# Bias times edge count between two graph layers: from additions on VectorE to one-row products on TensorE

## What is computed

```python
h = relu(layernorm(x))
# layer 0
ef  = (relu(edge_attr @ We1 + be1) @ We2 + be2) * sigmoid(ts @ Wt + bt)
msg = relu(concat([h[src], ef]) @ Wn1 + bn1) @ Wn2 + bn2
x   = x + segment_sum(msg, dst) + h
# layer 1
h   = relu(layernorm(x))
agg = segment_sum(h[src], dst)
x   = x + relu(relu((h + agg) @ W1 + b1) @ W2 + b2)
```

## Time and profile before

| | |
|---|---|
| median of 3 runs | 2862.56 us (2857.91 to 2863.95) |
| the profiled execution | 2860.48 us, span 2858.7 us, mean granted TensorE clock 0.892 |
| busy share of the span: PE, DVE, ACT, POOL | 84%, 69%, 35%, 73% |
| the stage between the layers, from the last sum to the scales | 2089.1 to 2123.9 us |

### The profile page before, as it was taken

One profiled execution on the slowest core, in us unless ns is written; L12 is line 12 of the kernel. 1 busy time (PEld: TensorE's weight loads), 2 busy tenths in 40 slices (PEclk: granted clock), 3 DMA queues, 4 the chain that ended last, 5 costly groups with the idle time before them and its releaser, 6 DMA issues.

```text
span 2858.7 us, 51515 instructions
## 1 busy us (share of the span) xinstructions
PE 2413.2 (84%) x14584; PEld 1509.5 (53%) x14585; DVE 1970.6 (69%) x4063; ACT 1001.7 (35%) x1000; POOL 2098.3 (73%) x2125
## 2 busy tenths in 40 slices
PE   5698899888889888988998898998846988877887
PEld 3455455545555555555554554554443666655665
DVE  7887767776777777777777777889886443444443
ACT  4344444444444444444443443443251111111113
POOL 7777777777777777777777777777737777777772
PEclk8899999999999999999999998999876788777878
DMA  6455554554545454555445544454314554455442
GB/s 224 117 161 158 155 156 155 155 154 155 155 154 155 154 155 155 154 155 155 154 154 155 154 155 150 155 156 144 103 67 151 163 163 149 135 163 162 150 131 69
DMA packets 229337, 426.09 MB, mean 149 GB/s; under 512 B 82703, under 2 KB 141664, under 8 KB 228992
## 3 DMA queue, kind: packets, MB, share of 16 engines
q0 software_dynamic: 74672, 152.51, 20.4%
q1 hardware_dynamic: 103152, 177.42, 18.5%
q10 hardware_dynamic: 51266, 93.34, 9.2%
HBM read 363.63 MB, written 59.43 MB: 148 GB/s over the span
## 4 chain that ended last, share of the span: by engine, by line
POOL 39%; PE 25%; issue 17%; DVE 10%; DVEq 5%; DMA 2%; ACT 1%; POOLq 0%; ACTq 0%; SPq 0%
POOL big L541 39%; PE ps L943 10%; PE ps L854 4%; PE ps L812 3%; PE ps L822 2%; DVE arena L1203 2%; PE ps L833 2%; DVE nodes L1203 2%; PE ps L933 1%; DVEq L1137 1%; PE ps L803 1%; DMA big<-table,idx 1%; DVEq L1183 1%; DVEq L1200 1%; DVEq L1203 1%
## 5 line engine op out<-in xcount | busy, mean ns | idle before, releaser
L541 POOL DMA_INDIRECT big<-table,idx x2080 | 2032.6, 977 | 658.1 <-issue 631.0
L656 ACT ACTIVATE big<-big 128x1024 f32<-128x1024 f32 x196 | 207.3, 1058 | 1014.7 <-DVE big L1152 1009.5
L854 PE MATMUL ps<-nodes 128*128 128x500 bf16 x1280 | 384.1, 415 | 180.1 <-DVE nodes L1203 179.2
L1152 DVE TENSOR_TENSOR big<-ps,big 128x1024 f32<-128x1024 f32 x196 | 239.8, 1224 | 328.6 <-DMA big<-table,idx 327.4
L1203 DVE TENSOR_SCALAR nodes<-iota_k,win_off,nodes 128x500 bf16<-128x500 f16 x1280 | 461.9, 413 | 0.0
L812 PE MATMUL ps<-arena,we 128*128 128x512 f32 x784 | 442.5, 692 | 11.8 <-DVE arena L1172 5.4
L833 PE MATMUL ps<-hot,big 128*128 128x64 f32 x3136 | 372.1, 272 | 1.6 <-DVE hot L1158 1.6
L833 PEld LDWEIGHTS ps<-hot,big 128*128 128x128 f32 x3136 | 365.9, 192 | 1.9 <-ACT big L656 1.7
L735 ACT ACTIVATE arena<-ps 128x490 f32<-128x490 f32 x96 | 100.1, 1043 | 557.0 <-PE ps L857 531.3
L854 PEld LDWEIGHTS ps<-nodes 128*128 128x128 bf16 x1280 | 95.6, 101 | 374.6 <-DVE nodes L1203 311.5
L646 ACT ACTIVATE arena<-ps,cols 128x1024 f32<-128x1024 f32 x196 | 218.5, 1115 | 202.7 <-PE ps L803 146.7
(11 more groups left out here) (147 smaller groups left out, 2382.3 us busy)
## 6 DMA issues: line engine op xcount, KB each, us to landing
arena<-in_ew SPq DMA_DIRECT2D x196, 512.0 KB
arena<-in_ea SPq DMA_DIRECT2D x196, 256.0 KB, 2.9
counts_d<-arena ACTq DMA_DIRECT2D x192, 245.0 KB
acc<-counts_d ACTq DMA_DIRECT2D x15, 2940.0 KB
big<-table,idx POOLq DMA_INDIRECT x2080
table<-big SPq DMA_DIRECT2D x7, 672.0 KB, 3.0
idx<-in_src SPq DMA_DIRECT2D x260, 4.0 KB, 1.6
xs<-in_x SPq DMA_DIRECT2D x7, 448.0 KB, 6.2
```

The lines of the kernel that those rows point to most:

```text
L541: pool.indirect_dma_start(to(u, q, t)[0:n], None, table, bass.IndirectOffsetOnAxis(ap=idx[0:n, u, at:at + 1], axis=0))\
L854: m = pe.matmul(to, hots[:, t, :], keys[:, t, :], start=False, stop=True, skip_group_check=True)
L1152: dve.tensor_tensor(msg[:, u % 2, :, :, :].rearrange("p q t d -> p (q t d)"), p_pre2, rows[:, u, :, :, :].rearrange("p q t d -> p (q t d)" ...
```

## The change

The bias additions on DVE go, with the seven multiplications on POOL, the count transfer on SP, the tile `count_n` and the four `biases` buffers. In their place:

- POOL copies the count row into a row `edge_counts` in partition 0, in which the 128 counts of a column lie side by side: seven copies of 7 x 128 elements. It waits for the last sum, no longer for a transfer.
- PE follows each of the 49 products by one with a single row, counts (1 x 128) by bn2 (1 x 128), in float32, which adds into the same PSUM buffer. Each group waits for its copy.
- SP waits for the last product before it loads the stored counts, as they overwrite the count row.

```diff
+        edge_counts = arena[0:1, at:at + N_PAD].rearrange("f (t p) -> f t p", t=NT)
...
             sp.wait_ge(acc_added, sweeps * NB)
-            sp.dma_start(count_n[:, :], acc[0:1, 1, 0:N_PAD].rearrange("a (p t) -> a p t", t=NT)).then_inc(counts_moved, 16)
-
-            sp.wait_ge(counts_moved, 16)
+            sp.wait_ge(upd_mm, NG)
             for i in (0, 1):
                 sp.wait_ge(c_stored[i], 16 + 16 * (NW0 // 2))
             load_sums(sp, 0)
...
-            pool.wait_ge(counts_moved, 16)
-            bn2_g = bn2_r[:, :].rearrange("p (a d) -> p a d", a=1).to_broadcast([P, GT, D])
+            pool.wait_ge(acc_added, sweeps * NB)
+            pool.sem_inc(pairs_begun, 1)
             for g in range(NG):
-                if g >= len(biases):
-                    pool.wait_ge(x1_chain, g - len(biases) + 1)
-                n = count_n[:, g * GT:(g + 1) * GT].rearrange("p (t a) -> p t a", a=1).to_broadcast([P, GT, D])
-                pool.tensor_tensor(biases[g % len(biases)], bn2_g, n, ALU.mult).then_inc(bias_made, 1)
+                pool.tensor_copy(edge_counts[:, g * GT:(g + 1) * GT, :], acc_group(g, 1)[0:1, :, :]).then_inc(counts_turned, 1)
             pool.tensor_copy(keys1, keys0).then_inc(keys_moved, 1)
...
                 if g >= 2:
                     pe.wait_ge(x1_made, g - 1)
+                pe.wait_ge(counts_turned, g + 1)
                 for u in range(GT):
-                    i = pe.matmul(p_prod[g % 2][:, u, :], stages[g % 2][:, u, :], wn2[:, :], start=True, stop=True)
+                    pe.matmul(p_prod[g % 2][:, u, :], stages[g % 2][:, u, :], wn2[:, :], start=True, stop=False)
+                    i = pe.matmul(p_prod[g % 2][:, u, :], edge_counts[:, g * GT + u, :], bn2_r[0:1, :], start=False, stop=True)
                 i.then_inc(upd_mm, 1)
...
-            def add_bias(g):
-                x_g = xs[:, g * GT:(g + 1) * GT, :]
-                dve.wait_ge(bias_made, g + 1)
-                dve.tensor_tensor(x_g, x_g, biases[g % len(biases)], ALU.add).then_inc(x1_chain, 1)
-
-            add_bias(0)
             for g in range(NG):
                 x_g = xs[:, g * GT:(g + 1) * GT, :]
                 dve.wait_ge(upd_mm, g + 1)
-                dve.wait_ge(x1_chain, g + 1)
                 dve.tensor_tensor(x_g, x_g, p_prod[g % 2], ALU.add).then_inc(x1_made, 1)
-                if g < NG - 1:
-                    add_bias(g + 1)
                 dve.wait_ge(x1_made, g + 1)
```

More of the change, by code:

```diff
@@ L122, in gnn_program @@
         rstd = sb("rstd", [P, NT])
-        count_n = sb("count_n", [P, NT])
         shift = sb("shift", [P, NT])
@@ L177, in gnn_program @@
         dense_edges = arena[:, at:at + NTILE]
+        edge_counts = arena[0:1, at:at + N_PAD].rearrange("f (t p) -> f t p", t=NT)
+        assert at + N_PAD <= sum(sizes) + 2 * BLK
         at += CB * CSUM
@@ L219, in gnn_program @@
         h_stages = [big[:, i * GT * D:(i + 1) * GT * D].rearrange("p (t d) -> p t d", t=GT) for i in (0, 1)]
-        biases = [big[:, i * GT * D:(i + 1) * GT * D].rearrange("p (t d) -> p t d", t=GT) for i in range(4)]
-        assert 4 * GT * D <= RROW
         half_at = RROW + 2 * TB * D - GT * D
@@ L304, in gnn_program @@
         acc_staged = sem("acc_staged")
-        counts_moved = sem("counts_moved")
-        bias_made = sem("bias_made")
-        x1_chain = sem("x1_chain")
         acc_zeroed = sem("acc_zeroed")
@@ L332, in gnn_program @@
         keys_moved = sem("keys_moved")
+        counts_turned = sem("counts_turned")
         sums_loaded = sem("sums_loaded")
```

## The result

The changed kernel takes 2903.97 us, the median of four runs between 2901.42 and 2907.02, beside 2863.26 us for the kernel before, now the median of four runs: a ratio of 1.0143, 95% interval 1.0127 to 1.0158. It is 40.7 us slower; 41 had been forecast.

The account below looks back on a forecast made before the run. VectorE was taken as the bound; TensorE's 98 products at 0.70 us, 68.6 us from 2093.97 us, plus 2.6 us of VectorE end at 2165.2 instead of 2123.9 us: 41 us more, 2904 us, range 2873 to 2914.

Parts of the forecast that it names:

- VectorE bounds, TensorE has 6 us of slack, 9 us to win: Stage between the layers: VectorE is the bound; without its bias additions it could end about 9 us earlier at most.
- A product with its change costs 0.70 us at half clock, 0.42 at full: TensorE's alternating 128-row and one-row products: 98 of them take 68.6 us at half clock, 41 us at full.
- TensorE starts as before, at 2093.97 us: Start of the stage: TensorE's branch past the skipped sweep loop sets it; the wait for GpSimd's first copy costs nothing.
- A change to 64 rows and one to a single row wait alike: TensorE's row changes: going from 128 rows to 64 or to one starts the next record 0.09 to 0.15 us late.
- Half clock for the whole stage: TensorE in the stage: pauses, 40% of the time without columns, keep the granted clock at 0.50; chance 0.62.
- the counting stretch: Cited evidence, 2188.2 to 2211.9 us: TensorE works through counts with pauses and was granted 0.50 for all 23.7 us.
- The full-clock rival: TensorE gets full clock after 4 to 5 us and keeps it: 15.7 us more, 2878 us; chance 0.22.
- No price for the change of rows: Rival: one-row products on TensorE follow like any other, 0.11 us a record: 3.7 us less, 2859 us; chance 0.12.
- GpSimd's copies at 0.80 to 2.53 us, hidden: Seven strided count-row copies, each 0.80 to 2.53 us, nearer the second; TensorE's wait on them costs nothing.
- SP's late load, hidden: SP's load of stored sums starts 2.6 us before the statistics end, is in about 7 us after, and costs nothing.
- VectorE waits some 7 us for a group: Sign in the profile after: VectorE waits for TensorE in six of seven groups, some 7 us each.
- The rest moves by the same amount: All behind the stage, scales, normalizing, table and gathers, moves by the same 41 us.

Follow-up runs that it names:

- the 64-row stream: Changed kernel with count products on 64 rows, alternating with 128: 2905.39 us begun cold; 2890.57 us begun warm behind 42 added 128-row products.
- the one-row run: Changed kernel with each group's seven 128-row products before its seven one-row products, plus 42 warming and 98 unbroken one-row products ahead of the first group: 2917.39 us.
- the grouped order: Changed kernel with each group's seven 128-row products first, then its seven one-row products, 2 changes of rows a group instead of 14: 2863.97 us, ratio 1.0014.

## Why the prediction was right, step by step

- *VectorE bounds, TensorE has 6 us of slack, 9 us to win.* Right: without the one-row products the stage lost 10.2 us.
- *A product with its change costs 0.70 us at half clock, 0.42 at full.* Right: 0.72 and 0.42 us. TensorE's stretch is 70.93 us where 68.6 were forecast. What made the sum 2.3 us too small is mostly the second record of a product: 0.34 us behind the first in the earlier trace rows, 0.38 us here. The weight loads of a product start together with its first record (PEld below), so they were not made ahead. The late start after a change was right, 0.35 us behind the last record for the forecast 0.21 + 0.15. TensorE's single records in the timeline of after show both:

```profile
2098.66 0.42 PE L904 MATMUL ps<-bn_r,arena 1*128 1x128 f32 x1
2099.00 0.50 PEld L903 LDWEIGHTS ps<-wn,big 128*128 128x128 f32 x2 [0.22 <-issue]
2099.00 0.58 PE L903 MATMUL ps<-wn,big 128*128 128x128 f32 x1
...
2099.38 0.42 PE L903 MATMUL ps<-wn,big 128*128 128x128 f32 x1
2099.73 0.58 PE L904 MATMUL ps<-bn_r,arena 1*128 1x128 f32 x1
```

  Against the 0.43 and 0.22 us of the products without a change, one change is worth 0.72 - 0.43 = 0.29 us at half clock and 0.42 - 0.22 = 0.20 at the full one.
- *TensorE starts as before, at 2093.97 us.* This term was too large by about as much. The first product stood 2093.97 - 2089.13 = 4.8 us behind ScalarE's first copy before and 2096.14 - 2093.23 = 2.9 us now; the branch began 0.8 us behind that copy then and 1.0 us ahead of it in this execution. So 2.3 us too little and 1.9 too much nearly cancel, and that the forecast met the median so closely is partly luck.
- *A change to 64 rows and one to a single row wait alike.* Right: 70.90 and 70.93 us. That the price could be avoided by using 96 or 128 rows was not in the prediction.
- *Half clock for the whole stage.* Right in its number, 0.50 over 70.93 us, and at most half right in its reason. The step laid it to the pauses, and the counting stretch stood for it. That a stream with pauses can stay cold fits the 64-row stream, cold against warm, but there the pauses are not parted from the 64 rows. And the prediction weighed only pauses: it did not see that one-row work loses the clock without any, as the one-row run did. With 56 changes instead of 98 the clock still stayed down. So the right level came in part from a reason that the runs don't bear out.
- *The full-clock rival's argument that the clock would stay once reached*. Wrong for this change (lost after 5.9 us), right for 64 rows (kept for 40.8 us). The Trainium skill, TensorE: Matmul & The Clock Gate, section Why this matters for your kernels, asks that TensorE be kept busy without a break and that long idle gaps be avoided; the prediction named the second alone. By the profile the one-row run met both, busy for 36.15 of 36.15 us, and was at half clock, so here the measurement decides against reading them as enough.
- *No price for the change of rows.* Refuted for 64 rows and for one; with 96 or 128 rows it is what happens, 2861 and 2860 us, near the 2859 of that rival.
- *GpSimd's copies at 0.80 to 2.53 us, hidden.* 1.76 us each, about the middle rather than near the upper end; the first was in 0.8 us before the branch was through.
- *SP's late load, hidden.* It started at 2167.15 us, 2.5 us before the statistics ended, as forecast. The first store of the table came 10.5 us after the statistics, at 2180.20 us, as before.

```profile
2180.20 0.34 SPq L471 DMA_DIRECT2D table<-big  x1
```

- *VectorE waits some 7 us for a group.* 7.55 us. *The rest moves by the same amount*: 41.7 us in the stage, 40.7 in the medians.

What stays open: how much of the 64-row stream's half clock in its cold run is due to the pauses and how much to the 64 rows, as no run of 64 rows without pauses began cold; how many rows between 1 and 64 are enough to keep the clock; where between 64 and 96 rows the change begins to cost; and when the grouped order reaches the full clock.

## What to carry to other kernels

Before small products are put between large ones on TensorE, look at the rows that both use: pad the small operand with zeros (96 and 128 rows were tried), or do all of one kind before the other. Padding brought the 41 us back in every run; the order did so in the median, but three of its runs were 15 to 19 us longer, and behind one-row work its clock stayed at half. Judge the granted clock of a stretch by its own row and not by PE's busy share, which was full at half clock throughout. And work that leaves the bound engine wins only what its new place leaves: VectorE's additions were worth 10 us here, and even in the cheap form TensorE's second products took 7 of them (a stage of 31.9 us, 2087.56 to 2119.49, beside 24.5 without bias and 34.8 before).

## What the runs showed of the hardware

- A dense run of one-row products, PE and its weight loads busy throughout, lost the full clock after 3.1 us; one with 64 rows kept it for 22 us.
- Groups of seven products on 128 rows and seven on one row were granted 1.00 from 3.6 us after a start behind 4.0 us of idleness, and 0.51 for 43 us behind a run of one-row products at half clock.
- One and the same stream (128 and 64 rows in turns) was granted 0.50 for 70.9 us when it began cold and 1.00 for 40.8 us when it began warm.
- A product of 96 rows behind one of 128 pays for no change (0.22 us from start to start at the full clock); one of 64 rows costs 0.20 us more, and so does one of a single row.
- A float32 product of one row by 128 columns takes as long as one of 128 rows: 0.11 us for a record at the full clock, 0.21 at half.
